# The last four slots of an attention stage: outputs two units back, weighed values last, rounding and statistics moved

## The chip, the cores and the metric

The kernel runs on one core of a Trainium2 chip. The metric is device time in microseconds of one execution. The kernel before was timed three times: 1239.37, 1240.72 and 1241.39 us, median 1240.72. A profiled execution of it, from which all rows below come, took 1239.88 us; its span, from the first to the last instruction, is 1238.6 us.

## What is computed

x has shape (2, 512, 512): two sequences of 512 tokens, 512 channels. Three blocks are added to it in turn:

```python
x = x + 0.5 * ffn(layernorm(x))       # silu(x A') * (x B'), times D'; A', B', D' are w * (su @ sv)
x = x + attn(layernorm(x))
x = x + 0.5 * ffn(layernorm(x))

# attn: 32 query heads in 8 groups, one key and one value head each, head width 128
q, k = rmsnorm(x @ Wq.T), rmsnorm(x @ Wk.T);  v = x @ Wv.T
scores = q @ k.T / sqrt(128) + slope * (key - query)    # masked where key > query
out = softmax(scores) @ v
return out @ Wo.T
```

Everything is float32. Each large matrix product is done as three products of rounded parts (high x high, low x high, high x low).

## The kernel before

One program is written out for each engine by hand: `tensor_program`, `scalar_program`, `vector_program`, `pool_program` and `sync_program`. An engine executes its own program in the order in which it is written; semaphores tie the programs together. Nothing else sets the order.

A tile is 128 tokens. In the attention, a unit is one tile of one of the 8 groups: 64 units (`UNITS`), numbered by group, then sequence, then tile. Unit 60 is the first tile of the second sequence in the last group and sees one block of 128 keys; 61, 62 and 63 see two, three and four. For each unit n there is a slot on each engine. The stages of a unit are these; "rounding" is ScalarE's copy of the high part from PSUM, and "the rest" is VectorE's subtraction that gives the low part and frees the bank.

- `turn_rows(n)`: TensorE transposes the normed query and key rows (L569, L572), ScalarE rounds them (qT_h, kT_h), VectorE makes the rest (qT_l, kT_l).
- `scores(n)`: 12 matmuls on TensorE (L345 to L347, kT and qT); VectorE adds the bias and takes the top of each of four heads (L1346).
- `exponentials(n)` on ScalarE (L961, four heads), `invert_sums(n)` on VectorE (L1351, one reciprocal that waits for the fourth head), `probabilities(n)` on ScalarE (L970, four heads by the inverse).
- `turn_probabilities(n)`: TensorE transposes prob (L590, four for each block of keys; in the first block head by head as ScalarE delivers), ScalarE rounds (probT_h, L976), VectorE makes the rest (probT_l, L1357).
- `weigh_values(n)`: TensorE multiplies with the values (L604, L605, L609); ScalarE rounds (oT_h, L981), VectorE makes the rest (oT_l, L1363).
- `project_out(n)`: 12 matmuls with the output weights (o_h, o_l); VectorE adds the result to the row of x (L1372).

There is one buffer each of qT, prob, probT and oT, and there are eight PSUM banks, taken in turn. In the slot of unit n the kernel works on the scores of n, the weighed values and the output of n-1, and the turned rows of n+1. Rows are projected four units ahead (`LEAD`); in the last four slots, 60 to 63, there is nothing left to project.

Work of the third block lies in these slots too. `output_statistics(u)` on VectorE is one statistics instruction (L1081) over the finished row of unit u; `normal_roots(2, 0)` is the layer norm's inverse roots for the first sequence, eleven short steps and an aggregate; GpSimd's `normalize(2, 0)` then makes xn (L1524), which TensorE turns in `turn_normed(2, 0)`. `split(1, 0, ...)` on ScalarE rounds the third block's first weights, blocks a11, a12, a21, a22, d0 and d1; GpSimd makes the rest of each in slots 60, 61 and 62. The first products of the third block are `gate_up(1, 0, 0, 0)`. GpSimd's order and SyncE's order are not touched by the change.

## Time and profile before

| what | value |
|---|---|
| median of three runs | 1240.72 us |
| the profiled execution | 1239.88 us |
| its span | 1238.6 us |
| TensorE busy | 1217.7 us, 98% |
| VectorE busy | 827.4 us, 67% |
| ScalarE busy | 757.3 us, 61% |
| GpSimd busy | 649.4 us, 52% |
| last four slots begin (scores of unit 60 on TensorE) | 973.58 us |
| first gate product of the third block begins | 1017.17 us |

The last two rows are start times within the span. "Busy" counts the time in which an instruction of the engine was under way; matmuls overlap, so a matmul of 0.39 us can start 0.23 us after the one ahead of it.

### The profile page before, as it was taken

The page shows a single profiled execution, that of the slowest core. Times are in us where ns is not written, and L with a number is a line of the kernel's source. Part 1 is how long each engine was busy: PE and PEld are TensorE (multiplying, and loading weights), DVE is VectorE, ACT ScalarE, POOL GpSimd, SP SyncE. Part 2 cuts the span into 40 slices and gives each one's busy share as a digit, 9 for nine tenths or more (in the row PEclk, how much of TensorE's full clock was granted, in tenths as well). Part 3 has the DMA queues.
Part 4 walks back from the last instruction along what each step waited for, and adds up shares of the span by engine and source line. Part 5 has one row for each costly group of instructions (what it writes and reads, how often), then busy time and mean ns, then how long its engine had stood idle before and what let it go on. Part 6 is the DMA issues. An engine that isn't in the chain of part 4 may idle for free.

```text
span 1238.6 us, 18593 instructions
## 1 busy us (share of the span) xinstructions
PE 1217.7 (98%) x6418; PEld 1067.7 (86%) x6418; DVE 827.4 (67%) x2002; ACT 757.3 (61%) x1760; POOL 649.4 (52%) x526
## 2 busy tenths in 40 slices
PE   6999999999999999999999999999999999999999
PEld 5788888899998999999999999999999778888887
DVE  7966665776666677567667667677677768655555
ACT  4454442357677777777767767767767774544442
POOL 4686561744675625725724724824824343765550
PEclk9999999999999999999999999999999999999999
DMA  6142232212213122122122122122122010221101
GB/s 232 40 156 106 105 104 102 93 44 86 70 51 103 43 77 102 41 80 95 43 85 94 43 86 94 44 86 87 51 86 77 26 51 19 63 74 52 52 17 68
DMA packets 33452, 93.77 MB, mean 76 GB/s; under 512 B 4112, under 2 KB 4784, under 8 KB 31312
## 3 DMA queue, kind: packets, MB, share of 16 engines
q1 hardware_dynamic: 33120, 92.29, 21.6%
q8 instruction: 52, 0.85, 0.3%
q14 instruction: 40, 0.33, 0.1%
q10 hardware_dynamic: 240, 0.30, 0.1%
HBM read 62.69 MB, written 29.88 MB: 75 GB/s over the span
## 4 chain that ended last, share of the span: by engine, by line
PE 90%; DVE 5%; ACT 2%; POOL 1%; issue 1%; DMA 1%; SPq 0%; DVEq 0%; ACTq 0%; POOLq 0%
PE bank L345 21%; PE bank L347 21%; PE bank L346 20%; PE bank L590 5%; PE bank L424 4%; PE bank L430 4%; PE bank L425 4%; PE bank L604 3%; PE bank L609 3%; PE bank L605 3%; PE bank L569 2%; DVE stats L1081 1%; PE bank L572 1%; PE bank L373 1%; DVE probT_l L1357 0%
## 5 line engine op out<-in xcount | busy, mean ns | idle before, releaser
L961 ACT ACTIVATE prob<-prob,neg_top 128x128 f32<-128x128 f32 (+3 forms) x256 | 141.1, 553 | 78.6 <-DVE neg_top L1346 78.0
L1603 POOL TENSOR_TENSOR rows<-rows,row_root_y 128x640 f32<-128x640 f32 x64 | 80.7, 1261 | 205.0 <-DVE row_root_y L1077 205.0
L1597 POOL TENSOR_TENSOR square<-rows 128x640 f32<-128x640 f32 x64 | 79.4, 1256 | 161.0 <-DVE rows L1382 125.1
L970 ACT ACTIVATE prob<-prob,inverse 128x128 f32<-128x128 f32 (+3 forms) x256 | 123.0, 553 | 5.5 <-DVE inverse L1351 5.5
L1472 POOL TENSOR_TENSOR w_l_late<-raw_late,w_h_late 128x512 fp32r<-128x512 f32 (+1 forms) x59 | 90.4, 1549 | 68.2 <-ACT w_h_late L718 68.2
L1357 DVE TENSOR_TENSOR probT_l<-bank,probT_h 128x512 fp32r<-128x512 f32 x160 | 101.4, 683 | 22.2 <-ACT probT_h L976 22.1
L976 ACT CAST probT_h<-bank 128x512 fp32r<-128x512 f32 x160 | 84.5, 595 | 43.0 <-PE bank L590 43.0
L1346 DVE CUSTOM_DVE_ANT_0 prob<-bank,bias 128x128 f32<-128x128 f32 (+3 forms) x256 | 109.7, 484 | 0.0
L345 PE MATMUL bank<-o_h,oT_h 128*128 128x512 f32 x256 | 105.6, 413 | 4.0 <-DVE oT_l L1363 4.0
L1142 DVE SCALAR_TENSOR_TENSOR x_rows<-bank,x_rows 128x512 f32<-128x512 f32 x112 | 75.7, 687 | 45.8 <-PE bank L430 45.8
L347 PE MATMUL bank<-o_h,oT_l 128*128 128x512 f32 x256 | 101.4, 396 | 0.0
L346 PE MATMUL bank<-o_l,oT_h 128*128 128x512 f32 x256 | 100.5, 393 | 0.0
L1382 DVE TENSOR_TENSOR rows<-bank,rows 128x384 f32<-128x384 f32 x72 | 40.0, 556 | 79.7 <-ACT rows L925 51.3
L345 PE MATMUL bank<-kT_h,qT_h 128*128 128x128 f32 (+3 forms) x256 | 86.5, 338 | 1.4 <-DVE qT_l L1333 1.4
L347 PE MATMUL bank<-kT_h,qT_l 128*128 128x128 f32 (+3 forms) x256 | 82.2, 321 | 0.0
L346 PE MATMUL bank<-kT_l,qT_h 128*128 128x128 f32 (+3 forms) x256 | 82.1, 321 | 0.0
L590 PE MATMUL bank<-ident,prob 128*128 128x128 f32 x640 | 80.2, 272 | 0.0
L590 PEld LDWEIGHTS bank<-ident,prob 128*128 128x128 f32 x640 | 73.9, 140 | 3.8
L1472 POOL TENSOR_TENSOR w_l_early<-raw_early,w_h_early 128x512 fp32r<-128x512 f32 x37 | 49.6, 1357 | 41.9 <-ACT w_h_early L718 41.8
L1363 DVE TENSOR_TENSOR oT_l<-bank,oT_h 128x512 fp32r<-128x512 f32 x64 | 44.2, 691 | 29.8 <-ACT oT_h L981 29.8
L604 PE MATMUL bank<-probT_h,v_h 128*128 128x512 f32 x160 | 63.8, 399 | 0.4 <-ACT probT_h L976 0.4
L605 PE MATMUL bank<-probT_h,v_l 128*128 128x512 f32 x160 | 62.8, 392 | 0.0
(213 smaller groups left out, 3751.6 us busy)
## 6 DMA issues: line engine op xcount, KB each, us to landing
x_ring<-x_between SPq DMA_DIRECT2D x64, 256.0 KB, 2.6
x_between<-x_ring SPq DMA_DIRECT2D x56, 256.0 KB, 2.0
raw_late<-w_qkv SPq DMA_DIRECT2D x8, 1536.0 KB, 6.5
raw_early<-ffn_w SPq DMA_DIRECT2D x21, 512.0 KB, 4.1
scaled<-raw_early SPq DMA_DIRECT2D x21, 512.0 KB, 2.7
raw_late<-scaled SPq DMA_DIRECT2D x21, 512.0 KB, 3.8
raw_late<-w_o SPq DMA_DIRECT2D x8, 1024.0 KB, 5.1
x_between<-x_rows SPq DMA_DIRECT2D x8, 256.0 KB, 2.0
```

The lines of the kernel that those rows point to most:

```text
L345: pe.matmul(bank, lh, rh, start=first, stop=False, skip_group_check=more)
L346: pe.matmul(bank, lh, rl, start=False, stop=False, skip_group_check=more)
L347: return pe.matmul(bank, ll, rh, start=False, stop=last, skip_group_check=more)
L590: last = pe.transpose(bank[:, h * P:(h + 1) * P], prob[:, h, j * P:(j + 1) * P], ident[:, :])
L604: pe.matmul(bank[:, :], v_h[:, b, j, :], turned[2 * j], start=j == 0, stop=False)
L605: pe.matmul(bank[:, :], v_l[:, b, j, :], turned[2 * j], start=False, stop=False)
L961: last = act.activation(p, p, ACT.Exp, bias=neg_top[:, h:h + 1], scale=-1.0, accum_out=total[:, h:h + 1])
L970: act.activation(p, p, ACT.Copy, scale=inverse[:, h:h + 1]).then_inc(prob_done, 1)
L976: act.copy(probT_h[:, j, :, :], banks[r.bank][:, :].rearrange("p (h q) -> p h q", h=G)).then_inc(probT_hi_done, 1)
L1346: dve.tensor_tensor_reduce(prob[:, h, 0:keys], banks[r.bank][:, 0:keys], bias[:, h, S - keys:S], -(2.0 ** -g), -MASKED, ALU.add, ALU.min, ...
L1357: dve.tensor_tensor(probT_l[:, j, :, :], banks[r.bank][:, :].rearrange("p (h q) -> p h q", h=G), probT_h[:, j, :, :].bitcast(F32), ALU.sub ...
L1472: return pool.tensor_tensor(lo, raw, hi.bitcast(F32), ALU.subtract)
```

## The change

In the slots of units 60 to 63 each of three engines gets another order.

TensorE: after the scores of n comes the output of unit n-2 (from slot 61 on), then the turned rows of n+1, then the weighed values of n-1, then, in slot 63, the turned xn, and the turned probabilities of n. The output of unit 62 follows the last slot.

ScalarE: the four exponentials stand together; in slot 60 the rounding of turned rows comes ahead of the scaled heads, in slots 61 and 62 behind them; the rounding of the weighed values follows. The weight blocks a11 and a12 are rounded in slot 60 as before, a21 and a22 at the end of slot 60 instead of slot 61, d0 and d1 after the weighed values of unit 63 instead of slot 62.

VectorE: the reciprocal comes ahead of the weighed values; the statistics of units 56, 57 and 58 come at the end of slot 60, of 59 at the end of slot 61 with the roots behind it, of 60 and 61 at the end of slot 63, of 62 ahead of the last output.

```diff
@@ tensor_program, slot @@
                 scores(n)
+                if ahead >= UNITS:
+                    if ahead > UNITS:
+                        project_out(n - 2)
+                    if n + 1 < UNITS:
+                        turn_rows(n + 1)
+                    weigh_values(n - 1)
+                    if n == UNITS - 1:
+                        turn_normed(2, 0)
+                    turn_probabilities(n)
+                    return
                 if n:
                     weigh_values(n - 1)
...
             for n in range(UNITS):
                 slot(n)
+            project_out(UNITS - 2)
             weigh_values(UNITS - 1)
@@ scalar_program @@
+            def late_slot(n):
+                exponentials(n, range(G))
+                if n == UNITS - LEAD:
+                    turn_rows(n + 1)
+                probabilities(n)
+                if UNITS - LEAD < n < UNITS - 1:
+                    turn_rows(n + 1)
+                weigh_values(n - 1)
+                if n == UNITS - LEAD:
+                    values_hi(n + 2)
+                    split(1, 0, "a11", "a12")
+                if n == UNITS - 1:
+                    turn_normed(2, 0, (0, 1))
+                turn_probabilities(n)
+                if n == UNITS - LEAD:
+                    split(1, 0, "a21", "a22")
+                if n == UNITS - 1:
+                    turn_normed(2, 0, (2, 3))
...
             weigh_values(UNITS - 1)
+            split(1, 0, "d0", "d1")
@@ vector_program @@
+            def late_slot(n):
+                scores(n)
+                if n == UNITS - LEAD:
+                    sum_squares(n + 2)
+                    sum_squares(n + 3)
+                invert_sums(n)
+                if n > UNITS - LEAD:
+                    project_out(n - 2)
+                if n + 1 < UNITS:
+                    turn_rows(n + 1)
+                if n == UNITS - LEAD:
+                    pair_roots(n + 2)
+                weigh_values(n - 1)
+                if n == UNITS - 1:
+                    turn_normed(2, 0, (0, 1))
+                turn_probabilities(n)
+                if n == UNITS - 1:
+                    turn_normed(2, 0, (2, 3))
+
+                for u in {UNITS - 4: (UNITS - 8, UNITS - 7, UNITS - 6), UNITS - 3: (UNITS - 5,), UNITS - 1: (UNITS - 4, UNITS - 3)}.get(n, ()):
+                    output_statistics(u)
+                if n == UNITS - 3:
+                    normal_roots(2, 0)
...
             for n in range(UNITS):
                 slot(n)
+            project_out(UNITS - 2)
             weigh_values(UNITS - 1)
+            output_statistics(UNITS - 2)
             project_out(UNITS - 1)
-            output_statistics(UNITS - 2)
             output_statistics(UNITS - 1)
```

In both of the lower programs the branches of the old `slot` that served the last four units are gone, and `slot` calls `late_slot` from unit 60 on.

On TensorE, around the weighed values of unit 60 in slot 61 (L345 to L347 with o and oT are an output, L569 and L572 the turned rows of unit 62, L604 to L609 the weighed values; - is before, + is now):

```order
+L347 MATMUL bank<-o_h,oT_l 128x512
+L569 MATMUL bank<-ident,rows 128x128 x4
+L572 MATMUL bank<-ident,rows 128x128
 L604 MATMUL bank<-probT_h,v_h 128x512
 L605 MATMUL bank<-probT_h,v_l 128x512
 L609 MATMUL bank<-probT_l,v_h 128x512
-L569 MATMUL bank<-ident,rows 128x128 x4
-L572 MATMUL bank<-ident,rows 128x128
-L345 MATMUL bank<-o_h,oT_h 128x512
-L346 MATMUL bank<-o_l,oT_h 128x512
-L347 MATMUL bank<-o_h,oT_l 128x512
```

The output that stood behind the weighed values, and needed them, is now that of the unit ahead and stands in front of them.

On ScalarE in slot 60, before, from the exponentials of unit 60 to those of unit 61:

```order
L961 ACTIVATE prob,total<-prob,neg_top 128x128 x4
L981 CAST oT_h<-bank 128x512
L970 ACTIVATE prob<-prob,inverse 128x128 x4
L949 ACTIVATE qT_h<-bank,q_scale 128x512
L953 CAST kT_h<-bank 128x128
L941 CAST v_h<-rows 128x128 x2
L718 CAST w_h_late<-raw_late 128x512 x2
L976 CAST probT_h<-bank 128x512
L961 ACTIVATE prob,total<-prob,neg_top 128x256 x2
```

And now (line numbers are those of the changed file):

```order
L970 ACTIVATE prob,total<-prob,neg_top 128x128 x4
L958 ACTIVATE qT_h<-bank,q_scale 128x512
L962 CAST kT_h<-bank 128x128
L979 ACTIVATE prob<-prob,inverse 128x128 x4
L990 CAST oT_h<-bank 128x512
L950 CAST v_h<-rows 128x128 x2
L727 CAST w_h_late<-raw_late 128x512 x2
L985 CAST probT_h<-bank 128x512
L727 CAST w_h_late<-raw_late 128x512 x2
L970 ACTIVATE prob,total<-prob,neg_top 128x256 x4
```

The rounding of the turned rows moved ahead of the heads and that of the weighed values behind them; a second pair of weight blocks came in.

On VectorE in slot 61, before, from the last score of unit 61 to the first of unit 62 (eight more short steps of the roots are left out):

```order
L1346 ISA neg_top 128x1
L1081 BN_STATS stats<-x_rows 128x6
L1363 TENSOR_TENSOR oT_l<-bank,oT_h 128x512
L1351 RECIPROCAL inverse<-total 128x4
L1086 BN_AGGR mv<-stats 128x2 x4
L1068 TENSOR_SCALAR ln_root_m<-mv 128x4
...
L1077 SCALAR_TENSOR_TENSOR ln_root_y<-ln_root_b,ln_root_y 128x4
L1333 SCALAR_TENSOR_TENSOR qT_l<-bank,q_scale,qT_h 128x512
L1338 TENSOR_TENSOR kT_l<-bank,kT_h 128x128
L1372 TENSOR_TENSOR x_rows<-bank,x_ring 128x512
L1357 TENSOR_TENSOR probT_l<-bank,probT_h 128x512 x2
L1346 ISA prob,neg_top<-bank,bias 128x384
```

And now:

```order
L1371 ISA neg_top 128x1
L1376 RECIPROCAL inverse<-total 128x4
L1397 TENSOR_TENSOR x_rows<-bank,x_ring 128x512
L1358 SCALAR_TENSOR_TENSOR qT_l<-bank,q_scale,qT_h 128x512
L1363 TENSOR_TENSOR kT_l<-bank,kT_h 128x128
L1388 TENSOR_TENSOR oT_l<-bank,oT_h 128x512
L1382 TENSOR_TENSOR probT_l<-bank,probT_h 128x512 x2
L1106 BN_STATS stats<-x_rows 128x6
L1111 BN_AGGR mv<-stats 128x2 x4
L1093 TENSOR_SCALAR ln_root_m<-mv 128x4
...
L1102 SCALAR_TENSOR_TENSOR ln_root_y<-ln_root_b,ln_root_y 128x4
L1371 ISA prob,neg_top<-bank,bias 128x384
```

The statistics and the roots moved from between the scores and the rest of the turned rows to the place right ahead of the scores of unit 62.

## Rows read from the trace of the kernel before

**Rows 1.** The page, busy time of each engine, its share, instructions.

```profile
PE 1217.7 (98%) x6418; PEld 1067.7 (86%) x6418; DVE 827.4 (67%) x2002; ACT 757.3 (61%) x1760; POOL 649.4 (52%) x526
```

**Rows 2.** Waits of TensorE, 973 to 1018 us: releaser, total, times, longest.

```profile
PE bank L345 <- DVE oT_l L1363: 4.0, 3, 2.0
```

**Rows 3.** Timeline of TensorE: start, length, instruction, count, idle before it.

```profile
979.34 0.50 PE L345 MATMUL bank<-o_h,oT_h 128*128 128x512 f32 x1 [0.85 <-DVE oT_l L1363]
...
982.18 0.60 PE L590 MATMUL bank<-ident,prob 128*128 128x128 f32 x4
...
987.43 0.50 PE L345 MATMUL bank<-o_h,oT_h 128*128 128x512 f32 x1 [1.98 <-DVE oT_l L1363]
...
992.66 0.42 PE L345 MATMUL bank<-kT_h,qT_h 128*128 128x384 f32 x1
...
998.08 0.50 PE L345 MATMUL bank<-o_h,oT_h 128*128 128x512 f32 x1 [1.13 <-DVE oT_l L1363]
...
1002.20 0.47 PE L345 MATMUL bank<-kT_h,qT_h 128*128 128x512 f32 x1
...
1017.17 0.47 PE L345 MATMUL bank<-xnT_hi,w_h_late 128*128 128x512 f32 x1 [0.60 <-DVE xnT_lo L1118]
```

**Rows 4.** Stretches: bounds, length, busy by engine, granted clock, DMA share, GB/s.

```profile
987.43:988.30 0.87, 0.87 (x4) 0.74 (x5) 0.59 (x6) 0.62 (x3) 0.00 (x0) 1.00 0.00 0
988.30:991.70 3.40, 3.40 (x10) 2.62 (x9) 2.52 (x13) 3.06 (x8) 1.28 (x1) 0.51 0.00 0
```

**Rows 5.** Timeline of VectorE, slots 60 to 62.

```profile
976.42 1.54 DVE L1320 TENSOR_REDUCE sums<-square 128x5 f32<-128x640 f32 x2
...
979.29 0.14 DVE L1068 TENSOR_SCALAR row_root_m<-sums 128x10 f32<-128x10 f32 x1
...
981.40 0.74 DVE L1333 SCALAR_TENSOR_TENSOR qT_l<-bank,q_scale,qT_h 128x512 fp32r<-128x512 f32 x1
...
984.04 0.69 DVE L1081 BATCH_NORM_STATS2 stats<-x_rows 128x6 f32<-128x512 f32 x1
984.64 0.41 DVE L1346 CUSTOM_DVE_ANT_0 prob<-bank,bias 128x256 f32<-128x256 f32 x1
...
987.77 0.35 DVE L1086 BATCH_NORM_AGGREGATE mv<-stats 128x2 f32<-128x6 f32 x4
...
990.22 0.75 DVE L1333 SCALAR_TENSOR_TENSOR qT_l<-bank,q_scale,qT_h 128x512 fp32r<-128x512 f32 x1
...
994.33 0.55 DVE L1346 CUSTOM_DVE_ANT_0 prob<-bank,bias 128x384 f32<-128x384 f32 x1
```

**Rows 6.** Timeline of ScalarE, slots 60 to 62.

```profile
977.37 0.18 ACT L961 ACTIVATION_READ_ACCUMULATOR prob<-prob,neg_top 128x1 f32 x1
...
980.60 0.67 ACT L949 ACTIVATE qT_h<-bank,q_scale 128x512 fp32r<-128x512 f32 x1
...
981.31 0.50 ACT L941 CAST v_h<-rows 128x128 fp32r<-128x128 f32 x2
981.71 1.14 ACT L718 CAST w_h_late<-raw_late 128x512 fp32r<-128x512 f32 x2
...
985.09 0.51 ACT L961 ACTIVATE prob<-prob,neg_top 128x256 f32<-128x256 f32 x1 [1.69 <-DVE neg_top L1346]
...
985.60 0.49 ACT L961 ACTIVATE prob<-prob,neg_top 128x256 f32<-128x256 f32 x1
...
987.89 1.70 ACT L970 ACTIVATE prob<-prob,inverse 128x256 f32<-128x256 f32 x4 [0.25 <-DVE inverse L1351]
...
998.15 2.14 ACT L970 ACTIVATE prob<-prob,inverse 128x384 f32<-128x384 f32 x4 [0.24 <-DVE inverse L1351]
```

**Rows 7.** Timeline of GpSimd, the third block's first layer norm.

```profile
990.42 8.31 POOL L1524 TENSOR_SCALAR xn<-x_rows,mv,ln_root_y 128x512 f32<-128x512 f32 x4 [3.05 <-DVE ln_root_y L1077]
```

**Rows 8.** Timelines of TensorE and ScalarE behind the slots.

```profile
1032.55 0.48 PE L424 MATMUL bank<-w_h_late,d_hi 128*128 128x512 f32 x1
...
1062.87 1.14 ACT L718 CAST w_h_late<-raw_late 128x512 fp32r<-128x512 f32 x2
```

More of the change, by code:

```diff
@@ L981, in weigh_values @@
                 act.copy(oT_h[:, :, :], banks[r.bank][:, :].rearrange("p (h q) -> p h q", h=G)).then_inc(oT_hi_done, 1)
+            def late_slot(n):
[16 more added lines that the diff above has]
+                    turn_normed(2, 0, (2, 3))
             def slot(n):
                 g, at = divmod(n, B * TB)
-                soon = G // 2 if unit(n)[2] == 1 else G if unit(n)[2] == 0 or n + LEAD < UNITS else G - 1
+                if n >= UNITS - LEAD:
+                    late_slot(n)
+                    return
+                soon = G // 2 if unit(n)[2] == 1 else G
                 exponentials(n, range(soon))
@@ L996, in slot @@
                     take_sum(ahead, 1) if n % 2 == 0 else take_sum(ahead - 1, 7)
-                if n + 1 < UNITS:
-                    turn_rows(n + 1)
+                turn_rows(n + 1)
                 if n % 2 == 0 and paired(n + 2):
@@ L1002, in slot @@
                     project_right(ahead)
-                elif ahead >= UNITS and n < UNITS - 1:
-                    split(1, 0, *(("a11", "a12"), ("a21", "a22"), ("d0", "d1"))[ahead - UNITS])
                 splits = QKV_WHEN[g + 1 >= SEVEN_FROM].get(at, ()) if g < HKV - 1 else ()
@@ L1389, in output_statistics @@
                 statistics(b * TB + t)
+            def late_slot(n):
[7 more added lines that the diff above has]
+                if n + 1 < UNITS:
+                    turn_rows(n + 1)
+                if n == UNITS - LEAD:
[10 more added lines that the diff above has]
+                    normal_roots(2, 0)
             def slot(n):
-                late = n + LEAD >= UNITS
+                ahead = n + LEAD
+                if ahead >= UNITS:
+                    late_slot(n)
+                    return
                 scores(n)
-                ahead = n + LEAD
                 if ahead - 1 < FIRST_PAIRED:
                     sum_squares(ahead - 1)
-                if ahead == UNITS:
-                    sum_squares(n + 2)
-                    sum_squares(n + 3)
-                if n == UNITS - 3:
-                    output_statistics(n - 2)
-                first = late or unit(n)[2] == 1
+                first = unit(n)[2] == 1
                 if n and first:
@@ L1408, in slot @@
                     weigh_values(n - 1)
-                if n % 2 == 0 and paired(n + 2) and ahead < UNITS:
+                if n % 2 == 0 and paired(n + 2):
                     sum_squares(n + 2)
                     sum_squares(n + 3)
-                if n % 2 == 0 and n + LEAD - 2 < UNITS:
+                if n % 2 == 0:
                     pair_roots(n + LEAD - 2)
-                if n == UNITS - 3:
-                    normal_roots(2, 0)
                 if paired(ahead):
                     add_products(ahead, 2) if n % 2 == 0 else add_products(ahead - 1, 5)
-                if n + 1 < UNITS:
-                    turn_rows(n + 1)
-                if unit(n - 2)[0] == HKV - 1 and n not in (UNITS - LEAD, UNITS - 3):
-                    output_statistics(n - 2)
+                turn_rows(n + 1)
                 if ahead < FIRST_PAIRED:
                     values_lo(ahead)
-                if n == UNITS - 1:
-                    turn_normed(2, 0, (0, 1))
-                elif n:
+                if n:
                     project_out(n - 1)
```

13 lines of the change are left out of this document (removed).

## The prediction

> **What bounds the kernel now.** I read the page first: TensorE is busy for 98% of the span, so only its idle or slowed microseconds can be won, and work added to its queue costs nothing here because none is added [rows 1]. Then the waits of TensorE in the attention's last four slots, from 973.5 us on: nearly all of them are three waits for oT_l, 4.0 us together [rows 2]. Then its timeline: the three waits stand ahead of the outputs of units 59, 60 and 61 (0.85, 1.98 and 1.13 us), and 0.60 us for xnT_lo stands ahead of the first gate product [rows 3]. Behind the 1.98 us wait the granted clock was 0.51 for 3.40 us, the lower level of 1.2 GHz, after full clock in the stretch before it [rows 4]. TensorE was busy throughout it, so 3.40 x (1 - 0.51) = 1.7 us went to the clock. All that could be won there is 3.96 + 0.60 + 1.7 = 6.3 us.
>
> What ends last is not TensorE's order but a chain through VectorE and ScalarE. In each slot VectorE reduces the four score banks, ScalarE takes four exponentials, VectorE one reciprocal, ScalarE scales four heads, and only then can TensorE turn them. I follow this chain under the new order.
>
> **The change on TensorE.** It removes and adds no TensorE instruction. Slots 60 to 63 run scores, output of n-2, turned rows, weighed values of n-1, turned probabilities; so the outputs of 59, 60 and 61 move one slot later, and that of 62 stands ahead of the weighed values of 63 as before. An output is 12 matmuls, 979.34 to 982.18, 2.84 us. The statistics of units 56 and 57 leave the slots 58 and 59 and land, with 58, behind the rounding of slot 60; the roots of the first half's layer norm go from ahead of the turned rows of 61 to the end of slot 61, ahead of the scores of 62.
>
> **Slot 60, step by step.** Up to the exponentials nothing moves: scores are reduced by 976.4, exponentials end 977.6 [rows 5, 6]. VectorE's two sums last to 977.9 (1.54), the reciprocal to 978.1. ScalarE meanwhile rounds the turned rows of 61 (0.7 for both, as from 980.60 to 981.31 before, to 978.2), scales the heads (1.2, to 979.4), rounds the weighed values of 59 (0.57, to 980.0), v (0.4) and two weight blocks (1.04), to 981.3, and only then the turned probabilities, to 981.9. VectorE: rows' remainder to 979.0, roots 2.1, to 981.1, oT_l to 981.8, probT_l to 982.6, three statistics of 0.6 (1.8), to 984.3. Before, it began its scores of 61 at 984.64. So 0.3 us are won. TensorE waits some 0.9 us for the last heads and 0.75 for oT_l of 59 (981.9), ends that output at 984.8, the turned rows at 985.3, the weighed values of 60 at 986.1.
>
> **Slot 61.** VectorE starts the scores at 984.3 and ScalarE the exponentials 0.45 us later, as before; four of 0.51, without the rounding that stood between them, and the fourth's sum end at 986.9, reciprocal 987.2, heads (1.70) 988.8, rows of 62 rounded 989.5, their remainder on VectorE 989.6 to 990.4 [rows 5, 6]. TensorE, done at 986.1, turns heads as they come until 989.5 (2.5 us of it waiting), and waits another 1.0 for kT_l: scores of 62 at 990.5, against 992.66 before [rows 3]. But VectorE has a queue behind it: oT_l of 60 (0.6), probT_l twice (1.2), statistics (0.6), roots 2.45 (987.77 to 990.22 [rows 5]), which end at 990.4 + 0.6 + 1.2 + 0.6 + 2.45 = 995.25. Before, the same roots lay where ScalarE scaled heads and VectorE had nothing else to do: qT_l would have waited until 990.1 anyway (ScalarE's rounding of 62 ended then); that cover is gone. Scores of 62 therefore begin on VectorE at 995.25, before at 994.33. Who waits for that: ScalarE's exponentials, and through them TensorE.
>
> **Slot 62.** First exponential at 995.85 (0.6 behind the scores); four of some 0.6 end at 998.4, reciprocal 998.65, heads (2.14) 1000.75, rows of 63 rounded 1001.5 and their remainder 1002.4 [rows 5, 6]. TensorE runs scores (2.2), output 60 (2.84), turned rows and weighed values of 61 (2.0) from 990.5 to 997.6, then turns the heads as they come and the other eight blocks (0.9), done 1001.8, of 4.2 us some 2.9 waiting, and 0.6 more for kT_l. Scores of 63 start at 1002.5. Before: 1002.20 [rows 3]. So by this point the shorter waits for oT_l have bought nothing, 0.3 us is lost, and one output is owed: three stood ahead of it (59, 60, 61), now two.
>
> **From there to the first gate product** TensorE is the bound in both orders: before, 1002.20 to 1017.17 with one wait of 0.60 [rows 3]. Now 14.97 - 0.60 + 2.84 = 17.2 us. Cover of each wait inside: heads of 63 are needed at 1012.2; VectorE's scores start at 1004.8, exponentials end 1008.4, heads 1011.2, 1.0 us early; output 62 stands between the turned probabilities of 63 and their values, so xnT_lo and probT_l are no longer late (the 0.60 us is gone). The gate product starts at 1002.5 + 17.2 = 1019.7, 2.5 us late.
>
> **The clock.** The stretch from 997.6 to 1002.5 has 12 transposes and is otherwise idle; the one that preceded the slow stretch held a wait of 1.98 us [rows 3, 4]. That from 986.1 to 990.5 is as empty. A slow stretch behind the first is free: TensorE is done with the scores of 62 some 2.5 us before VectorE takes them. Behind the second it delays scores of 63 and the output, all on the path. Bounds: nothing, or the 1.7 us of before; half of it may lie over waiting transposes, so I take 1.1. Sum: 2.5 + 1.1 = +3.6 us.
>
> The Trainium skill's page "TensorE: Matmul & The Clock Gate" (section "Why this matters for your kernels") warns only of idle gaps between bursts of matmuls that are longer than any single one here. By that rule the drop of rows 4 would not stand where it does and the sum would be 2.5; by the row it is 3.6. The trace disagrees with the page, and I go by the trace.
>
> **What lies beside other work, at nothing.** The layer norm's four tiles on GpSimd start at 995.4 instead of 990.42 and take 8.31 us, to 1003.7; TensorE turns them at 1010.3 (6.6 us of cover) [rows 7]. Weight blocks a21 and a22 follow on GpSimd and are wanted some 20 us later. Blocks d0 and d1 are rounded behind the last oT_h, to about 1021.3 on ScalarE and some 3 us later on GpSimd, wanted by the first down product, 1032.55 before, about 1036 now [rows 8]. Silu's table load then comes about when the gate's half is done; VectorE wants silu only after the roots behind output 63. SyncE fetches the next step's down weights only after d1's remainder, from about 1024; ScalarE rounds them at 1062.87 [rows 8]. Statistics behind the last output are one fewer, 0.6 us, under gate products. If any cover failed, its price would be at most its lateness: none is within 1 us but silu's, which no one waits for.
>
> **Against the times.** The profiled execution took 1239.88 us (span 1238.6), 0.84 under the median of 1240.72. I add the sum to each: 1243.5 by that execution, 1244.3 by the median. I forecast the latter.
>
> **Rivals.** *No slow stretch on the path* (the page's rule above, or the chip's phase): +2.5, 1243.2. For it: the single waits in 997.6 to 1002.5 are shorter than 1.98 us, with transposes between. Against: rows 4. *Dearer clock*: a slow stretch wholly on scores and output of 63, and a further one at slot 60 that pushes the chain: 2.5 + 1.7 + 1.7 = +5.9, 1246.6. *Roots not on the chain*: if VectorE had 2.45 us free between probT_l of 61 and scores of 62, the sum is 3.6 - 2.45 = +1.2, about 1241.9. Against: those scores have lain in PSUM since 991, no idle time stands there. *Faster*: the waits for oT_l go and the heads come in time, so nothing replaces them: -3.96 - 0.60 - 1.7 = -6.3, 1234.4; with half of it given back, 1237.6. It decides if the heads of 61 and 62 were ready at 986.1 and 997.6; I find 988.8 and 1000.75. For it: an output two back really is always ready, and TensorE is 98% busy. Against: ScalarE and VectorE alternate without a gap that would let the heads be that early.
>
> **Numbers.** Chances: forecast 0.50 (own range 2.7 to 4.7 more, 1243.4 to 1245.4), no slow stretch 0.18, dearer clock 0.12, roots off the chain 0.13, faster 0.07. The range takes in the forecast, the no-slow-stretch case and most of the dearer one: 1241.6 to 1246.6. About 0.2% (2.5 us) is what a measurement of this kernel can tell from no change: faster by more 0.07; within, the roots case and two thirds of the no-slow-stretch case (it sits on the border), 0.25; slower by more 0.68.
>
> **What would show it.** Right: TensorE's waits for oT_l shrink to under 1 us, new ones stand ahead of turned probabilities (for prob) and scores (for kT_l), together some 7 to 8 us; VectorE's scores of 62 begin right behind the roots; three outputs of 12 matmuls run between the scores of 63 and the gate product; xn on GpSimd starts 4 to 5 us later. Wrong: VectorE idle ahead of the scores of 62, or scores of 63 starting a microsecond or more before 1002.5.

## The result, and the profile after

| | before | after |
|---|---|---|
| median | 1239.62 us (22 runs, 1237.78 to 1241.71) | 1241.74 us (22 runs, 1240.44 to 1243.38) |
| ratio, 95% interval | | 1.0017 [1.0011, 1.0023] |
| profiled execution, span | 1239.88 us, 1238.6 | 1243.35 us, 1242.0 |
| scores of unit 60 begin on TensorE | 973.58 us | 974.16 us |
| first gate product | 1017.17 us | 1020.69 us |
| between the two ("the stretch") | 43.59 us | 46.53 us |
| from the gate product to the end of the span | 221.4 us | 221.3 us |

The change costs about 2.1 us by the medians, 0.17%. The prediction, 1244.3, was 2.6 us too high; the time lies only 0.14 us above the lower end of the stated range and outside the forecast's own 1243.4 to 1245.4. The profiled execution of the changed kernel, 1243.35 us, is the second slowest of its 22 runs. What is changed lies in the stretch, 2.94 us longer; behind it nothing moved, and the 0.58 us ahead of it varies from execution to execution (over the 14 profiles of this case the scores of 60 began between 972.83 and 974.16).

The page first, the row that answers to [rows 1]:

```profile
PE 1219.0 (98%) x6418; PEld 1067.6 (86%) x6418; DVE 828.0 (67%) x2002; ACT 756.9 (61%) x1760; POOL 649.0 (52%) x526
```

The counts are the same to the instruction, so TensorE's 1.3 us more of busy time are not more work. The view of TensorE's waits, 973 to 1022 us (releaser, total, times, longest), against [rows 2]:

```profile
PE bank L590 <- ACT prob L979: 4.0, 5, 1.9
PE bank L345 <- DVE qT_l L1358: 0.8, 1, 0.8
PE bank L345 <- DVE oT_l L1388: 0.6, 1, 0.6
```

The waits for oT_l are gone but for one, and waits for the scaled heads stand in their place: 5.4 us in all against 4.6. The timeline of TensorE, the places of [rows 3] in the new order (start, length, instruction, count, idle before it):

```profile
982.47 0.50 PE L345 MATMUL bank<-o_h,oT_h 128*128 128x512 f32 x1 [0.63 <-DVE oT_l L1388]
...
988.28 1.87 PE L590 MATMUL bank<-ident,prob 128*128 128x128 f32 x8 [1.50 <-ACT prob L979]
990.99 0.41 PE L345 MATMUL bank<-kT_h,qT_h 128*128 128x384 f32 x1 [0.84 <-DVE qT_l L1358]
...
999.90 0.74 PE L590 MATMUL bank<-ident,prob 128*128 128x128 f32 x2 [1.89 <-ACT prob L979]
...
1002.93 0.76 PE L345 MATMUL bank<-kT_h,qT_h 128*128 128x512 f32 x1
1003.49 0.63 PE L346 MATMUL bank<-kT_l,qT_h 128*128 128x512 f32 x1
...
1005.57 0.39 PE L345 MATMUL bank<-kT_h,qT_h 128*128 128x512 f32 x1
1005.80 0.40 PE L346 MATMUL bank<-kT_l,qT_h 128*128 128x512 f32 x1
...
1020.69 0.39 PE L345 MATMUL bank<-xnT_hi,w_h_late 128*128 128x512 f32 x1
```

The reader is to see three things. The output (982.47) waits little. The probabilities of 61 and 62 are waited for (1.50 and 1.89), and inside the group of eight transposes at 988.28, which lasts 1.87 us, TensorE idles between heads too, some 0.8 us: in the kernel before, the same eight transposes came without a wait and took 1.04 (its row below). So this view of waits undercounts. And the first scores of 63 are slow: the first six stand 1002.93 to 1005.57 = 2.64 us, the next six 1.38.

```profile
991.87 1.04 PE L590 MATMUL bank<-ident,prob 128*128 128x128 f32 x8
```

The windows of the slow place in the kernel after (bounds, length, busy by engine, granted clock), as [rows 4]:

```profile
1001.00:1002.00 1.00, 0.82 (x7) 0.67 (x7) 0.12 (x1) 1.00 (x4) 1.00 (x1) 1.00 0.61 205
1002.00:1003.00 1.00, 0.91 (x6) 0.54 (x4) 1.00 (x3) 1.00 (x3) 1.00 (x2) 0.54 0.04 6
1003.00:1004.00 1.00, 1.00 (x3) 0.81 (x4) 1.00 (x3) 0.94 (x2) 1.00 (x1) 0.50 0.03 10
1004.00:1005.00 1.00, 1.00 (x4) 0.81 (x3) 1.00 (x3) 0.00 (x0) 1.00 (x2) 0.50 0.00 0
1005.00:1006.00 1.00, 1.00 (x4) 0.81 (x4) 1.00 (x4) 0.14 (x1) 1.00 (x2) 0.75 0.00 0
1006.00:1007.00 1.00, 1.00 (x6) 0.80 (x5) 1.00 (x3) 1.00 (x3) 0.79 (x1) 1.00 0.00 0
```

The granted clock fell to 0.50, the level of 1.2 GHz, some 2 us behind the wait of 1.89, and was back by 1006. I call this a slow stretch.

VectorE's timeline between the scores of 61 and those of 62, against [rows 5]:

```profile
984.85 0.41 DVE L1371 CUSTOM_DVE_ANT_0 prob<-bank,bias 128x256 f32<-128x256 f32 x1
...
992.60 0.68 DVE L1106 BATCH_NORM_STATS2 stats<-x_rows 128x6 f32<-128x512 f32 x1
993.31 0.38 DVE L1111 BATCH_NORM_AGGREGATE mv<-stats 128x2 f32<-128x6 f32 x4
...
995.71 0.16 DVE L1102 SCALAR_TENSOR_TENSOR ln_root_y<-ln_root_b,ln_root_y 128x4 f32<-128x4 f32 x1
995.79 0.55 DVE L1371 CUSTOM_DVE_ANT_0 prob<-bank,bias 128x384 f32<-128x384 f32 x1
```

No bracket stands on the last row: VectorE came to the scores of 62 straight from the roots, 4.8 us after TensorE had begun them. ScalarE's and GpSimd's timelines show who waited for that, as [rows 6, 7]:

```profile
996.39 0.62 ACT L970 ACTIVATE prob<-prob,neg_top 128x384 f32<-128x384 f32 x1 [4.88 <-DVE neg_top L1371]
```
```profile
995.99 8.29 POOL L1559 TENSOR_SCALAR xn<-x_rows,mv,ln_root_y 128x512 f32<-128x512 f32 x4 [8.28 <-DVE ln_root_y L1102]
```

### The profile page after: what moved, and what is told of

The parts are those of the page before. It is cut to its first block, busy times and chain, and to the rows that moved or that the text cites. A ratio compares the mean times of both kernels' runs of the same rounds, so it can differ in the third digit from the quotient of the medians.

```text
span 1242.0 us, 18593 instructions
## 1 busy us (share of the span) xinstructions
PE 1219.0 (98%) x6418; PEld 1067.6 (86%) x6418; DVE 828.0 (67%) x2002; ACT 756.9 (61%) x1760; POOL 649.0 (52%) x526
## 4 chain that ended last, share of the span: by engine, by line
PE 91%; DVE 4%; ACT 2%; POOL 1%; issue 1%; DMA 1%; SPq 0%; DVEq 0%; ACTq 0%; POOLq 0%
PE bank L345 21%; PE bank L347 21%; PE bank L346 21%; PE bank L590 5%; PE bank L424 4%; PE bank L430 4%; PE bank L425 4%; PE bank L604 3%; PE bank L609 3%; PE bank L605 3%; PE bank L569 2%; DVE stats L1106 1%; PE bank L373 1%; PE bank L572 1%; ACT prob L970 1%
## 5 line engine op out<-in xcount | busy, mean ns | idle before, releaser
L345 PE MATMUL bank<-o_h,oT_h 128*128 128x512 f32 x256 | 104.8, 409 | 0.6 <-DVE oT_l L1388 0.6
L347 PE MATMUL bank<-o_h,oT_l 128*128 128x512 f32 x256 | 100.8, 394 | 0.0
L345 PE MATMUL bank<-kT_h,qT_h 128*128 128x128 f32 (+3 forms) x256 | 87.0, 340 | 2.3 <-DVE qT_l L1358 2.3
L347 PE MATMUL bank<-kT_h,qT_l 128*128 128x128 f32 (+3 forms) x256 | 82.5, 322 | 0.0
L604 PE MATMUL bank<-probT_h,v_h 128*128 128x512 f32 x160 | 63.9, 399 | 0.3 <-ACT probT_h L985 0.3
```

Source lines behind the costliest of these rows:

```text
L345: pe.matmul(bank, lh, rh, start=first, stop=False, skip_group_check=more)
L347: return pe.matmul(bank, ll, rh, start=False, stop=last, skip_group_check=more)
L604: pe.matmul(bank[:, :], v_h[:, b, j, :], turned[2 * j], start=j == 0, stop=False)
```

## Experiments

The theory: TensorE's new order is good in itself; the loss is the statistics of three units and the roots, which now lie on the chain VectorE, ScalarE, TensorE of slots 60 to 62; and a slow stretch comes on top in some executions, at about 1.2 us where TensorE is the bound and nothing where it runs ahead of the chain. Rivals: the late weighed values or the order of TensorE are the loss; the roots have slack; the clock explains most of the 2 to 3 us.

Each row of the table has the kernel's median, the ratio to the kernel before on the same chip, the stretch of its profile, and the granted clock of its runs. The kernel before had a median of 1239.07 us beside the first four, 1240.10 beside the next four, 1239.39 beside the last four (27 runs each). Where its own runs had a clock of 1.0, it took 1239.02 (19 runs), 1239.19 (13) and 1239.07 (14), and at 0.999 it took 1240.5: the profiled one was of the latter kind.

| kernel | median us, runs | ratio [95%] | stretch us | clock of the runs |
|---|---|---|---|---|
| waits_filled | 1241.94, 11 | 1.0022 [1.0013, 1.0031] | 45.36 | 1.0 in all |
| roots_moved | 1239.79, 11 | 1.0005 [0.9997, 1.0014] | 43.68 | 0.997 to 1.0 |
| roots_twice | 1244.91, 5 | 1.0047 [1.0033, 1.0061] | 48.67 | 0.996, 0.997 |
| stats_back | 1241.16, 11 | 1.0018 [1.0009, 1.0027] | 44.59 | mostly 0.999 |
| before_filled | 1239.22, 11 | 0.9993 [0.9984, 1.0002] | 42.41 | 1.0 in all |
| both_moved | 1237.83, 11 | 0.9984 [0.9975, 0.9993] | 41.12 | 1.0 in all |
| after, again | 1242.18, 11 | 1.0018 [1.0009, 1.0027] | 46.49 | 0.997 to 0.999 |
| order_alone | 1257.30, 4 | 1.0127 [1.0105, 1.0148] | 61.04 | 0.990 to 0.996 |
| stats_back_filled | 1240.45, 11 | 1.0001 [0.9992, 1.0010] | 43.57 | 1.0 in all |
| roots_moved_filled | 1239.53, 11 | 0.9997 [0.9988, 1.0006] | 42.93 | 1.0 in all |
| tuned | 1236.90, 11 | 0.9981 [0.9972, 0.9990] | 40.45 | 1.0 in 10 of 11 |
| after, a third profile | 1242.09, 1 | | 45.35 | 0.999 |

### The clock: waits filled, in the kernel after and in the one before

In the kernel after, TensorE gets products that no one uses (o_h by o_h, into the bank that the next operation overwrites) ahead of the heads of 61 and 62, between heads, and ahead of the scores of 62:

```diff
+            def fill(bank, times, cols=512):
+                for _ in range(times):
+                    pe.matmul(bank[:, 0:cols], o_h[:, 0, 0:P], o_h[:, 1, 0:cols], start=True, stop=True, skip_group_check=True)
@@ turn_probabilities @@
+                    if j == 0:
+                        fill(bank, {61: 6, 62: 7}.get(n, 0))
+                            if h and n in (61, 62):
+                                fill(bank[:, h * P:(h + 1) * P], 1, P)
@@ scores @@
-                pe.wait_ge(evac[turned_q.bank], turned_q.nth)
-                pe.wait_ge(evac[turned_k.bank], turned_k.nth)
...
+                    if h == 0:
+                        fill(bank, {62: 3}.get(n, 0))
+                        pe.wait_ge(evac[turned_q.bank], turned_q.nth)
+                        pe.wait_ge(evac[turned_k.bank], turned_k.nth)
```

> The changed kernel with idle matmuls (high parts of the output weights with themselves, overwritten at once) in TensorE's waits: six ahead of the turned heads of 61, three ahead of the scores of 62, seven ahead of the turned heads of 62, a narrow one between heads. Theory of the clock: the granted clock stays at 1.0 from 973 to 1020 us, the slow stretch at 1002 us (1.2 us by the trace) goes, 1.0 to 1.2 us faster than the changed kernel. Rival (the slow stretch is free, or the filling delays the path by as much): within 0.4 us of it; if the fillers are late at a head, slower by up to 0.5 us.

And in the kernel before, eight of them ahead of the output of unit 60, where it waited 1.98 us:

```diff
@@ before, project_out @@
+                r, bank = result("out", n)
+                fill(bank, {60: 8}.get(n, 0))
                 pe.wait_ge(evac[weighed.bank], weighed.nth)
-                r, bank = result("out", n)
```

> The kernel before with eight idle matmuls (1.8 us) in TensorE's 1.98 us wait ahead of the output of 60, in the bank that this output then overwrites. Theory of the clock: no run has a slow stretch in the slots, every run takes what the runs at granted clock 1.0 take, 1239.0 us, and the runs near 1240.5 us are gone. Rival (the runs near 1240.5 us have another cause): both levels stay.

All 22 runs of the two had a clock of 1.0. None of before_filled took over 1239.65 us: the runs near 1240.5 are gone. The windows of the filled kernel after (columns as above):

```profile
974.00:990.00 16.00, 15.02 (x85) 11.85 (x84) 12.63 (x44) 12.63 (x39) 7.32 (x8) 1.00 0.07 16
990.00:1006.00 16.00, 14.89 (x75) 11.80 (x74) 12.26 (x42) 8.96 (x22) 10.37 (x6) 1.00 0.06 19
1006.00:1019.17 13.17, 13.17 (x77) 11.44 (x75) 9.33 (x20) 9.40 (x21) 0.43 (x1) 1.00 0.08 21
```

So at one and the same clock the change is 45.36 - 42.41 = +2.95 us, and by the runs 1241.94 - 1239.02 = 2.9 over the kernel before at a clock of 1.0. The slow stretch is worth 46.53 - 45.36 = 1.17 in the profile of after and 43.59 - 42.41 = 1.18 in that of before. The clock therefore does not make the loss; it is on both sides. By the medians, though, filling the kernel after won nothing: 1241.94 against 1241.74 (1242.18 in after_again), where 1.0 to 1.2 us had been expected. The 1.17 belongs to executions like the profiled one, which was among the slowest, and not to the median one; as for the time of the kernel, the rival came true. The medians of the two kernels differ by 2.1 rather than 2.9 because the kernel before has a slow stretch in some of its runs, and for one reason more that stays open (below).

### The kernel after twice more

> The changed kernel once more, for the granted clock of each execution beside its time and for a second trace. Theory: executions with two slow stretches (clock 0.997) take no longer than those with none (1242.0 us), since the first lies in the hole of slot 61, where TensorE is 2.5 us ahead of VectorE, and the second over waiting transposes; one that starts on the scores of 63 costs 1.2 us. Rival: each slow stretch costs 1.5 us, as in the kernel before, so 1245 with two.

> The changed kernel once more, for another profile of it. By the theory a slow stretch that falls on the turned probabilities and scores of 62 (TensorE ahead of the chain there) costs nothing and one on the scores of 63 costs 1.1 to 1.2 us: stretch 45.4 us in the first case, 46.5 in the second. Rival: every slow stretch costs about 1.2 us wherever it falls.

The second profile repeats the first: stretch 46.49, granted clock 0.54 from 1001.3 to 1005.0, on the scores of 63. Of the runs of after_again, the four with a clock of 0.997, two slow stretches by its size, took 1241.48 to 1243.05 us, median 1242.06, about what waits_filled takes; the rival's 1245 is out. The third profile has its slow stretch elsewhere. Its windows, and its first scores of 63 on TensorE:

```profile
986.00:989.90 3.90, 2.25 (x10) 1.23 (x10) 1.03 (x5) 3.65 (x13) 1.61 (x2) 0.96 0.12 33
989.90:993.00 3.10, 2.59 (x10) 2.22 (x9) 3.10 (x6) 1.52 (x4) 0.00 (x0) 0.50 0.11 43
993.00:1003.00 10.00, 8.22 (x43) 6.31 (x42) 6.27 (x29) 6.45 (x17) 7.10 (x4) 1.00 0.09 28
```
```profile
1002.84 0.47 PE L345 MATMUL bank<-kT_h,qT_h 128*128 128x512 f32 x1 [0.40 <-DVE qT_l L1358]
```

3.1 us at half the clock, on the scores of 62, and the stretch is 45.35 us, that of the filled kernel to 0.01: TensorE's later wait took it all up. In this kernel a slow stretch behind slot 61's hole costs nothing, behind slot 62's 1.2 us, by one and two profiles. The rival (1.2 wherever it falls) is out.

### TensorE's order alone

The order of TensorE from the change, ScalarE's from before, and VectorE's as near to before as the order allows.

```diff
@@ before, tensor_program, slot @@
+                if ahead >= UNITS:
+                    if ahead > UNITS:
+                        project_out(n - 2)
+                    if n + 1 < UNITS:
+                        turn_rows(n + 1)
+                    weigh_values(n - 1)
+                    if n == UNITS - 1:
+                        turn_normed(2, 0)
+                    turn_probabilities(n)
+                    return
```

> TensorE's new order alone; ScalarE keeps its old one and VectorE all but the output rows, statistics and roots, which follow the outputs (59, its statistics and the roots behind the reciprocal of 61). Theory (chain): ScalarE now waits for the weighed values, which TensorE makes later, in the middle of the exponentials, 2.3 us in slot 61, 3.9 in slot 62, 2.7 in slot 63; TensorE waits some 15 us in the slots; 10 to 11 us over the kernel before, 8 over the changed kernel. Rival (TensorE's order is the gain and the rest of the change the cost): faster than the kernel before.

It is 17.2 us slower than the kernel before by the medians, 15.7 by the ratio. ScalarE's timeline shows the lock, unit 61's second and third exponential with the rounding of oT_h between them:

```profile
986.34 0.49 ACT L972 ACTIVATE prob<-prob,neg_top 128x256 f32<-128x256 f32 x1
...
991.56 0.59 ACT L992 CAST oT_h<-bank 128x512 fp32r<-128x512 f32 x1 [4.64 <-PE bank L609]
992.04 0.51 ACT L972 ACTIVATE prob<-prob,neg_top 128x256 f32<-128x256 f32 x1
```

In the old order ScalarE rounds the weighed values after two of four exponentials. TensorE now weighs them last, so ScalarE stands for 4.64 us with work behind it that was ready (4.46 in slot 62, 3.81 in slot 63, where 2.3, 3.9 and 2.7 had been expected for the three), and TensorE then waits for its heads: 6.7 us for prob and 3.7 for qT_l from 974 to 1022 us. The expectation, 10 to 11 us over the kernel before, was some 6 short. The clock is the likely reason, since it was 0.55 from 981.5 to 988.0, 0.50 from 995.7 to 1002.0 (both below) and 0.50 from 1010 to 1016; no run with filled waits shows what it took here.

```profile
981.50:988.00 6.50, 5.13 (x19) 4.52 (x19) 4.20 (x16) 3.73 (x11) 5.63 (x6) 0.55 0.00 0
995.70:1002.00 6.30, 4.01 (x14) 3.81 (x13) 5.01 (x18) 3.53 (x9) 4.64 (x3) 0.50 0.03 12
```

The moves of ScalarE's roundings belong to TensorE's new order. The statistics and the roots are free to stand elsewhere, and so are the weight blocks.

### The roots

Moved from the end of slot 61 to behind the reciprocal of 62, where VectorE waits for the heads anyway; and, as the opposite, the eleven root steps done twice in their place.

```diff
@@ roots_moved, vector_program, late_slot @@
                 invert_sums(n)
+                if n == UNITS - 2:
+                    normal_roots(2, 0)
...
-                if n == UNITS - 3:
-                    normal_roots(2, 0)
@@ roots_twice @@
                 if n == UNITS - 3:
+                    for last in inverse_root(ln_roots, mv[:, 0:TB, 1], LN_EPS, slice(0, TB)):
+                        pass
+                    own_step(last)
                     normal_roots(2, 0)
```

> The changed kernel with one edit: the layer norm's roots (2.45 us on VectorE) stand behind the reciprocal of unit 62 instead of ahead of the scores of 62. Theory (the chain through VectorE and ScalarE sets the end): the scores of 62 on VectorE and everything behind them start 2.45 us earlier, the gate product 2.3 us earlier; about 2.2 us faster than the changed kernel, level with the kernel before or 0.2 us slower. Rival (TensorE's order with the outputs two back is what costs, the roots lie under other work): the time of the changed kernel, 2 us over the kernel before.

> The changed kernel with the eleven root steps ahead of the scores of 62 done once more, some 2.1 to 2.45 us on VectorE. Theory (chain): each microsecond there arrives at the end in full, so 2.1 to 2.4 us slower than the changed kernel, 4.2 to 4.6 us over the kernel before. Rival (VectorE has room there): within 0.5 us of the changed kernel.

> The roots taken out from ahead of the scores of 62, with waits filled, so at a granted clock of 1.0. By the theory (the roots lie on the chain for all of their 2.45 us, less some tenths that another wait takes over): 2.3 us under the changed kernel with filled waits, about 43.1 us of stretch and 1239.6 us, still 0.5 above the kernel before at that clock. Rival (half of what the roots' move gave was a better placed slow stretch): 44.2 us and 1240.8.

Twice the root steps: the stretch grew by 48.67 - 46.53 = 2.14 us, with 2.1 us of steps put in (in after they stand from 993.73 to 995.79). The two profiles can be compared, since both have a slow stretch on the scores of 63. That of roots_twice has one more, on the scores of 62, where it costs nothing (windows of roots_twice, columns as above):

```profile
990.30:994.20 3.90, 3.41 (x12) 3.44 (x13) 3.69 (x12) 1.01 (x3) 0.00 (x0) 0.56 0.00 0
1003.90:1008.60 4.70, 4.65 (x17) 3.58 (x16) 4.70 (x11) 2.78 (x8) 4.70 (x4) 0.64 0.02 3
```

Its median is 3.2 us over that of after and 5.8 over the kernel before, more than the 2.1 to 2.4 and 4.2 to 4.6 expected. All five of its runs had a clock of 0.996 or 0.997, so it may pay in each of them the 1.2 us that the median run of after does not; no filled version was run.

Moved away, with waits filled: VectorE began the scores of 62 19.03 us behind the start of the stretch instead of 21.63, and the stretch shrank from 45.36 to 42.93, by 2.43. The medians agree: 1241.94 - 1239.53 = 2.4. The scores of 62 on VectorE and the first gate product, in waits_filled (its stretch begins at 973.81) and in roots_moved_filled (972.83):

```profile
995.44 0.55 DVE L1381 CUSTOM_DVE_ANT_0 prob<-bank,bias 128x384 f32<-128x384 f32 x1
1019.17 0.39 PE L345 MATMUL bank<-xnT_hi,w_h_late 128*128 128x512 f32 x1
```
```profile
991.86 0.54 DVE L1381 CUSTOM_DVE_ANT_0 prob<-bank,bias 128x384 f32<-128x384 f32 x1
1015.76 0.39 PE L345 MATMUL bank<-xnT_hi,w_h_late 128*128 128x512 f32 x1
```

Both ways the roots count in full: they have no slack. Without filling, the profile of roots_moved had a clock of 0.52 for 7.1 us:

```profile
984.00:988.30 4.30, 2.75 (x14) 1.73 (x13) 2.47 (x11) 3.35 (x12) 3.11 (x3) 1.00 0.00 0
988.30:995.40 7.10, 6.75 (x22) 5.97 (x22) 5.42 (x14) 4.71 (x14) 0.00 (x0) 0.52 0.15 37
```

which explains why its stretch, 43.68, was 0.75 above that of the filled version. With the roots gone TensorE is less far ahead of VectorE, and a slow stretch on the scores of 62 is no longer free: TensorE turns the heads of 62 at 999.47 without a wait, that is, it comes last itself. The interval of roots_moved holds 1: its time cannot be told from that of the kernel before.

### The statistics

Those of 56 and 57 back in slots 58 and 59, that of 58 behind the row of 59 in slot 61.

```diff
+                if n == UNITS - 3:
+                    output_statistics(UNITS - 6)
...
-                for u in {UNITS - 4: (UNITS - 8, UNITS - 7, UNITS - 6), UNITS - 3: (UNITS - 5,), ...
+                for u in {UNITS - 3: (UNITS - 5,), ...
@@ slot @@
+                if n in (UNITS - 6, UNITS - 5):
+                    output_statistics(n - 2)
```

> The changed kernel with the statistics of units 56 and 57 back in the slots 58 and 59 and that of 58 behind the output row of 59 in slot 61: 1.8 us of VectorE's queue ahead of the scores of 61 gone. Theory (chain): scores of 61 begin 1.8 us earlier and so does the gate product; 1.8 us faster than the changed kernel, 0.3 us over the kernel before. Rival (the 0.3 us that slot 60 wins over before shows that statistics cost nothing there): no change.

> Statistics of 56 and 57 back in slots 58 and 59, with TensorE's waits filled by products that no one uses, so that the granted clock stays at 1.0 and the statistics are priced by themselves. By the theory (three statistics at the end of slot 60 push the whole chain of slots 61 and 62, until the scores of 63): 1.8 us under the changed kernel with filled waits, whose stretch from the scores of unit 60 to the first gate product is 45.36 us, so about 43.6 us and 1240.1 us. Rival (the statistics have slack, and the little that their return gave in the medians, 0.6 us, is all they are worth): 45 us and 1241.3.

Without filling, the profile said 46.53 - 44.59 = 1.9 us and the medians only 0.6, against 1.8 expected, which left it open whether the statistics matter (10 of the 11 runs of stats_back had a clock below 1.0, and their median is 0.7 over that of its filled version). The filled pair settles it: 45.36 - 43.57 = 1.79 us in the profiles, 1241.94 - 1240.45 = 1.5 in the medians. VectorE's scores of 62 (993.83 in a stretch that begins at 973.98, so 19.85 against 21.63) and everything after them came 1.8 us sooner, which is three statistics of 0.6.

### Both, and two steps further

> The changed kernel with both edits: roots behind the reciprocal of 62, statistics of 56 and 57 back in slots 58 and 59, that of 58 behind the output row of 59. Theory (chain): the two gains add, 2.3 + 1.8 = 4.1 us between the scores of 60 and the gate product; 1237.9 us where the changed kernel takes 1242.0 with no slow stretch, so 1.1 us faster than the kernel before (1239.0 in its runs with no slow stretch). Rival (each of the two only uncovers the other, TensorE's order has a floor of its own): 2.3 us at most, level with the kernel before.

Roots and statistics moved together give 41.12 us, which is 4.24 under the filled kernel after: 2.43 + 1.79 = 4.22, the two prices simply add. It beats the kernel before by little, but clear of the noise: 0.9984 [0.9975, 0.9993]. Its clock was 1.0 in every run, with nothing filled in. Its waits of TensorE, 974 to 1022 us:

```profile
PE bank L345 <- DVE qT_l L1358: 1.4, 2, 0.8
PE bank L345 <- DVE oT_l L1388: 0.6, 1, 0.6
PE bank L590 <- ACT prob L979: 0.4, 2, 0.3
```

No wait is over 0.84 us. VectorE has one thing left ahead of the scores of 62 that could stand elsewhere, the statistic of 59:

```profile
990.82 0.68 DVE L1106 BATCH_NORM_STATS2 stats<-x_rows 128x6 f32<-128x512 f32 x1
991.42 0.54 DVE L1371 CUSTOM_DVE_ANT_0 prob<-bank,bias 128x384 f32<-128x384 f32 x1
```

The last version moves it into VectorE's idle time behind the row of 59 (the expectation below says 60), and lets ScalarE round the turned probabilities of 60 ahead of blocks a11 and a12 (`A` is the four blocks a11 to a22):

```diff
@@ tuned, against both_moved @@
-                    split(1, 0, "a11", "a12")
...
-                    split(1, 0, "a21", "a22")
+                    split(1, 0, *A)
...
+                    output_statistics(UNITS - 5)
...
-                for u in {UNITS - 3: (UNITS - 5,), UNITS - 1: (UNITS - 4, UNITS - 3)}.get(n, ()):
+                for u in {UNITS - 1: (UNITS - 4, UNITS - 3)}.get(n, ()):
```

> The version with roots and statistics moved, and two more steps: the statistic of 59 stands right behind the sum of the row of 60 (off the end of slot 61), and blocks a11 and a12 are rounded with a21 and a22 behind the turned probabilities of 60, so that ScalarE rounds those 1.0 us sooner. By the theory (the chain of VectorE and ScalarE still sets the scores of 61 and 62, TensorE still waits 1.4 us for qT_l): 0.7 us less, stretch 41.1 us, about 1237.1 us. Rival (TensorE's own work is the bound by now): stretch 41.8 us, 1237.8 us, no change.

The stretch is 40.45, against the 41.12 of both_moved 0.67 less, as the theory had it. The two steps were not run apart; from the start of the stretch VectorE's scores of 61 came 0.1 us sooner and those of 62 0.7, so nearly all of it is the statistic. (The expectation's 41.1 and 41.8 took as both_moved's gate product one that begins 0.68 us after the first; both are too high by that, so the rival, no change, would have been 41.12.) The median is 1236.90 us, 0.9981 [0.9972, 0.9990] of the kernel before. As a gain over both_moved, each at its own chip's clock-1.0 runs of before, it is 1236.86 - 1239.07 = -2.21 against 1237.83 - 1239.19 = -1.36. Its row that answers to [rows 3], and its waits:

```profile
997.58 0.47 PE L345 MATMUL bank<-kT_h,qT_h 128*128 128x512 f32 x1 [0.58 <-DVE qT_l L1357]
```
```profile
PE bank L345 <- DVE qT_l L1357: 1.4, 2, 0.8
PE bank L345 <- DVE oT_l L1387: 0.6, 1, 0.6
PE bank L590 <- ACT prob L979: 0.3, 1, 0.3
```

TensorE still waits 2.3 us: the chain is the bound in slots 60 to 62 even here.

## Why the prediction was right, and where its sizes were off

In the first two paragraphs times of after are given less the 0.58 us by which its stretch began later.

**Slots 60 and 61: right.** VectorE's scores of 61 were forecast for 984.3 and came at 984.27. The scores of 62 began on TensorE at 990.41 (forecast 990.5) and on VectorE at 995.21 (995.25). The step on which the forecast turned, that the roots lose their cover and push the scores of 62, is shown by the runs: 2.43 us given back when they are moved, 2.14 lost when doubled.

**Slot 62: right.** Scores of 63 at 1002.35, forecast 1002.5, with a clean clock up to there (in the third profile 1002.84 - 0.49 = 1002.35 again).

**From there to the gate product: the mechanism right, the term too large.** It was 14.97 - 0.60 + 2.84 = 17.2 us. In the two filled kernels, at a clock of 1.0 throughout, the same piece is 1016.45 - 1001.53 = 14.92 us before (0.59 of it waiting) and 1019.17 - 1002.62 = 16.55 after. One output of 12 matmuls more stands in it (2.81), but four other terms shrank by 0.6 together. The pieces that shrank are those that stood next to a change between short transposes and long matmuls and no longer do, or less; that this is the cause is read from the table, no run tests it:

| piece | before, filled | after, filled |
|---|---|---|
| output behind the scores or the turned xn | 2.84 | 2.72 |
| weighed values of 62 | 2.04 | 2.04 |
| turned xn | 1.92 | 1.75 |
| turned probabilities of 63 | 1.71 | 1.67 |
| weighed values of 63, without the wait | 2.99 | 2.72 |

The forecast kept the durations of the old order for a new one. This term of the sum was 17.2 - 16.55 = 0.65 us too high.

**The clock: the price right, its place right by luck, the base wrong.** The forecast put 1.1 us of slow stretch on the path; it was 1.17 in the first profile and 0 in the third. For the kernel before it reckoned with 1.7 us lost to the clock; filled, it was worth 1.18, and 0.27 of the difference is the wait ahead of the output of 61, 1.13 us there and 1.40 filled. What it missed is that [rows 4] are a matter of the single execution: of 81 runs of the kernel before in the experiments 46 had a clock of 1.0. The profiled execution was one with a slow stretch, and so, by their times, were two of the three first runs. Their median, 1240.72, was 1.10 us over that of 22 runs, and this is the largest part of the 2.6 us by which the forecast missed the time. The rest is the 0.65 above and 0.8 that follows from taking a sum made between two executions with a slow stretch for one between two medians: the kernel before's median is 0.5 over its clean clock, and after's 0.3 under.

**The rival "no slow stretch", +2.5:** by size it came nearest to the medians (+2.1), but not by its reason; most runs of after had a clock of 0.997 to 0.999. The Trainium skill's page "TensorE: Matmul & The Clock Gate" (section "Why this matters for your kernels"), on which it rested, warns of single idle gaps longer than any in these slots. The runs disagree with it: behind a wait of 1.89 us, with short transposes around it, the granted clock was 0.50, and with the same waits filled it never fell.

**The rival "roots off the chain"** is refuted by roots_twice. **The rival "faster"** named the right condition, heads of 61 ready when TensorE has done the weighed values of 60. They were not, since VectorE was late; in tuned, with statistics and roots out of the way, the view has no wait for a head in slots 61 and 62 (the 0.3 us stand in slot 60; between the heads of 61 some 0.6 us is left, since its eight transposes take 1.67), and the time comes out 2 us under before.

**Costs put at nothing: right.** GpSimd's layer norm ended at 1004.3 in the trace of after, and TensorE turned xn at 1011.72. The gate product began without a wait. From it to the end it is 221.4 us in the kernel before and 221.3 in after, so the late d0 and d1, the silu table and the last statistics are all covered.

**Signs.** Of waits for prob and kT_l 7 to 8 us were forecast; the view shows 4.0 + 0.8. The forecast counted idle time between heads, which the view has inside the groups of transposes (0.8 us in the one at 988.28). The times at which the next work starts agree to 0.15 us, so it is the sign that was badly chosen. Another was miscounted: two outputs, those of 61 and 62, run between the scores of 63 and the gate product, and not three; the sum had it right with one more than before. The others came: the wait for oT_l is 0.6 us, the scores of 62 stand right behind the roots, and xn starts 5.0 us later (5.6 in the trace, less the 0.58).

**The chances.** Slower by more than 0.2% had 0.68, no change that can be told 0.25. The change is 0.17%, on the side that had 0.25; but 22 runs do tell it from none, [1.0011, 1.0023], so the 2.5 us that a measurement was held to need was too much. That the time lies in the range at all it owes in part to the range's width: the base was 1.10 us too high and the sum 1.5.

**Open.** Ten runs of after have a clock of 0.997, two slow stretches by its size, and take 1241.66, while runs at 1.0 take 1242.05 (2) and the filled kernel 1241.94. No profile caught after at 0.997, and why these are 0.3 us quicker is not known; in after_again the four at 0.997 had a median of 1242.06 and were not quicker. Three runs of after, at 0.998 and 0.999, took 1240.4 to 1240.6, below every filled one, which no profile explains either.

## What to carry over

When work is moved to an engine that is only 67% busy, look at what the engine does next: three statistics and a layer norm's roots cost their full 4.2 us because they stood ahead of a reduction that the next engine's whole slot hung on. A few steps away, behind the reciprocal or in VectorE's idle time, they cost next to nothing (with the roots moved the reduction came 2.60 us sooner and the gate product 2.43). A new order of the matmuls may be worth something (here 1.3 us at a full clock, 42.41 - 41.12, with the roundings that must go with it and whatever else of the change stayed in both_moved: the weight blocks and the reciprocal were not priced apart) and still come out slower, so price it apart from what travels with it. And before a sum made from one profile is set on a median, compare that profile's granted clock with those of several runs.

## What the runs showed of the hardware

The granted clock fell to 0.5 for about 3 to 4 us at a time (7.1 in roots_moved, some 6 three times in order_alone) shortly behind places where TensorE had waits of 1.5 to 2.7 us (2.68 in roots_twice, behind which it was 0.50), most of them among short transposes. The same program did this in some executions and not in others (the kernel before: a clock of 1.0 in 46 of 81 runs), at one place or another (the scores of 62 or of 63). Not every such wait brought it: behind the 1.50 us in slot 61 the profile of after has 1.00. It was never seen where the waits were filled with idle products (44 of 44 runs at 1.0; before_filled still had one wait of 1.40 us), and once where no wait was over 0.84 us (both_moved and tuned, 21 of 22 runs at 1.0). The products cost nothing measurable: before_filled took 1239.22 us against 1239.19 for the runs of the kernel before at full clock. Against all its runs the gain stays within the interval, 0.9993 [0.9984, 1.0002].
